# Perceiver block on one core: the order and the semaphores of the first loads, and the first norms group by group

## The reference, cut to what matters

```python
x = x + L0_xattn(_layernorm(x), ctx_1024, ...)   # self attention, cross attention, feed forward
x = x + L0_attn(_layernorm(x), ...)
x = x + L0_ffn(_layernorm(x), ...)
x = x + L1_xattn(_layernorm(x), ctx_1024, mask, ...)
x = x + L1_attn(_layernorm(x), ...)
x = x + L1_ffn(_layernorm(x), ...)
```

```python
scores = einsum('bhqd,bhkd->bhqk', q, q) / sqrt(128)
scores = where(among the 5 largest of the row, scores, -inf)
out = merge_heads(softmax(scores) @ q) @ self_out_w.T + self_out_b
x = layernorm(x + out) * ln1_g + ln1_b
```

## Time and profile before

| | |
|---|---|
| median of 3 runs | 3657.43 us (3654.14 to 3657.65) |
| the profiled execution, its own time | 3659.62 us |
| its span, first to last instruction | 3656.9 us |
| busy: PE, DVE, ACT, POOL | 92%, 69%, 52%, 31% of the span |
| mean granted TensorE clock | 0.958 |
| first instruction of DVE, PE, ACT | 15.86, 22.95, 24.24 us |

### The profile page before, as it was taken

How to read it: one execution, slowest core, us unless ns; L and a number is a source line. 1 busy time by engine, 2 the same in 40 slices (tenths; PEclk the granted TensorE clock), 3 DMA queues, 4 the chain that set the end, 5 groups by cost and what they waited for, 6 DMA issues and landing times. The chain is left out here.

```text
span 3656.9 us, 83216 instructions
## 1 busy us (share of the span) xinstructions
PE 3368.5 (92%) x32913; PEld 2372.4 (65%) x32913; DVE 2508.6 (69%) x7162; ACT 1895.5 (52%) x2944; POOL 1145.4 (31%) x807
## 2 busy tenths in 40 slices
PE   6879999999997787999999999999999998957998
PEld 4646666666665665777777777777777776634555
DVE  5657777778785444777777777777777776675333
ACT  4336666666664222666666666666666664522332
POOL 1043333333331003433444334443344431233000
PEclk9969999999999688999999999999999999978999
DMA  1023333333330011111111111111111101000000
GB/s 52 2 68 75 81 71 76 76 78 73 75 65 1 2 47 41 42 33 35 37 42 42 33 36 37 42 42 33 30 42 42 42 22 47 1 27 1 1 1 12
DMA packets 95125, 146.43 MB, mean 40 GB/s; under 512 B 14961, under 2 KB 72337, under 8 KB 93969
## 3 DMA queue, kind: packets, MB, share of 16 engines
q1 hardware_dynamic: 94736, 141.12, 14.4%
HBM read 100.66 MB, written 1.05 MB: 28 GB/s over the span
## 5 line engine op out<-in xcount | busy, mean ns | idle before, releaser
L2137 DVE SCALAR_TENSOR_TENSOR arena<-banks,arena 128x512 f16<-128x512 f32 (+1 forms) x1024 | 554.4, 583 | 309.2 <-ACT arena L2226 307.9
L2226 ACT ACTIVATE arena<-banks 128x512 f16<-128x512 f32 (+1 forms) x1024 | 471.4, 512 | 399.5 <-PE banks L2044 396.4
L1092 DVE TENSOR_REDUCE arena<-banks 128x1 f32<-128x512 f32 (+1 forms) x896 | 529.1, 627 | 187.1 <-PE banks L977 181.8
L1189 ACT ACTIVATE arena<-banks 128x1024 f32<-128x1024 f32 (+1 forms) x448 | 425.0, 964 | 315.1 <-PE banks L998 312.2
L2149 DVE CUSTOM_DVE_ANT_0 arena<-banks,arena 128x1024 f32<-128x1024 f32 (+1 forms) x512 | 494.3, 987 | 31.0 <-issue 30.7
L2233 ACT ACTIVATE arena<-arena 128x1601 f32<-128x1601 f32 x256 | 417.7, 1632 | 107.3 <-DVE arena L2155 105.3
L2044 PE MATMUL banks<-consts,arena 128*128 128x128 f32 (+1 forms) x3328 | 457.6, 276 | 7.4 <-DVE arena L2137 6.6
L2058 PE MATMUL banks<-arena 128*128 128x256 f16 (+1 forms) x1664 | 456.2, 274 | 0.7 <-ACT arena L2240 0.7
L2060 PE MATMUL banks<-arena 128*128 128x256 f16 (+1 forms) x1664 | 451.3, 271 | 0.0
L2059 PE MATMUL banks<-arena 128*128 128x256 f16 (+1 forms) x1664 | 450.2, 271 | 0.0
L2044 PEld LDWEIGHTS banks<-consts,arena 128*128 128x128 f32 (+1 forms) x3328 | 365.6, 141 | 17.6 <-issue 10.5
(11 more groups left out here) (364 smaller groups left out, 6144.6 us busy)
## 6 DMA issues: line engine op xcount, KB each, us to landing
arena<-in_ctxT SPq DMA_DIRECT2D x64, 800.5 KB, 4.5
arena<-arena SPq DMA_DIRECT2D x768, 50.0 KB, 2.2
arena<-in_ctx SPq DMA_DIRECT2D x32, 768.0 KB
arena<-in_mask SPq DMA_DIRECT2D x32, 200.1 KB, 4.5
arena<-in_m2w SPq DMA_DIRECT2D x3, 2048.0 KB, 8.4
arena<-in_xw SPq DMA_DIRECT2D x1, 2048.0 KB, 11.6
weights<-in_weights SPq DMA_DIRECT2D x1, 1920.0 KB, 7.7
arena<-in_ctx SPq DMA_DIRECT2D x32, 32.5 KB
```

The source lines that it names most:

```text
L1092: eng.tensor_reduce(o, s, AX, ALU.max).then_inc(a_max, 1)
L1189: eng.activation(pr[0:w, at % 4, :].rearrange("p (x n) -> p x n", x=2)[:, :, 0:n], c.ps[0:w, bank:bank + 2, 0:n], ACT.Exp, scale=scale).th ...
L2137: eng.scalar_tensor_tensor(out=part(ptl, g, gr), in0=turned(gr), scalar=TOP, in1=part(pth, g, gr), op0=ALU.mult, op1=ALU.subtract).then_in ...
L2226: eng.activation(part(pth, g, gr), turned(gr), ACT.Copy, scale=TOP).then_inc(t_high, 1)
```

## The change

It issues the loads in another order, `x` first and in two parts (pairs 0 to 3, then 4 to 15), then `consts`, `rows`, `weights`; gives each part of `x` and `consts` a semaphore of its own; takes the loads out of the `after` list; lets DVE wait for the two parts of `x`, PE for `consts` ahead of its first loop and for `rows` and `weights` ahead of the first projection; and interleaves DVE's statistics and norms: statistics of group g, then the norms of group g - 1.

```diff
-        c.loaded = ctx.enter_context(nc.semaphore("inputs_loaded"))
+        c.loaded = ctx.enter_context(nc.semaphore("weights_rows_loaded"))
+        c.x_loaded = [ctx.enter_context(nc.semaphore(f"x_loaded{n}")) for n in range(2)]
+        c.consts_loaded = ctx.enter_context(nc.semaphore("consts_loaded"))
...
     def sp(eng):
+        x = A["x"].rearrange("(i b) l d -> (b l) i d", b=2)
+        eng.dma_start(c.x[:, 0:G, :], x[:, 0:G, :]).then_inc(c.x_loaded[0], 16)
+        eng.dma_start(c.x[:, G:PAIRS, :], x[:, G:PAIRS, :]).then_inc(c.x_loaded[1], 16)
+        eng.dma_start(c.c[:], A["consts"]).then_inc(c.consts_loaded, 16)
+        eng.dma_start(c.r[:], A["rows"]).then_inc(c.loaded, 16)
         eng.dma_start(c.w[:], A["weights"]).then_inc(c.loaded, 16)
-        eng.dma_start(c.r[:], A["rows"]).then_inc(c.loaded, 16)
-        eng.dma_start(c.c[:], A["consts"]).then_inc(c.loaded, 16)
-        eng.dma_start(c.x[:], A["x"].rearrange("(i b) l d -> (b l) i d", b=2)).then_inc(c.loaded, 16)
...
-    m.after = [(c.loaded, 64), (constant, 5)]
+    m.after = [(constant, 5)]
...
         def project(g):
             eng.wait_ge(s["oT"], g + 1)
+            if g == 0:
+                eng.wait_ge(c.loaded, 32)
...
+        eng.wait_ge(c.consts_loaded, 16)
         for g in range(GROUPS):
             bank = 4 + g % 2
...
     def dve(eng):
-        norms.dve_stats(eng, lambda i: c.x[:, i, :])
-        for g in range(GROUPS):
-            norms.dve_apply(eng, g, lambda i: c.x[:, i, :], lambda i: xn[:, i, :])
+        for g in range(GROUPS + 1):
+            if g < GROUPS:
+                if g < 2:
+                    eng.wait_ge(c.x_loaded[g], 16)
+                norms.dve_measure(eng, g, lambda i: c.x[:, i, :])
+            if g > 0:
+                norms.dve_apply(eng, g - 1, lambda i: c.x[:, i, :], lambda i: xn[:, i, :])
```

## The result

The changed kernel took 3638.96 us (median of 5 runs, 3636.83 to 3640.58), the kernel before 3655.78 us (5 runs, 3649.94 to 3657.65): ratio 0.9956, 95% interval 0.9943 to 0.997, so 16.8 us less, with an interval of 11 to 21 us. Forecast were 13.5 us less and 3643.9 us; the time lies inside the range of 3638.5 to 3649.5, but only 0.5 us above its low end. The profiled execution took 3640.58 us at a span of 3638.8.

What follows compares the result with a forecast made beforehand. The start was taken to bound what the change can move: loads, POOL's memsets and operations, DVE's norm, then PE. PE's first transposes ending at 10.66 instead of 24.14 gave 13.5 us, from 3657.43 to 3643.9 us, range 3638.5 to 3649.5.

Steps and rivals of the forecast that it cites:

- The path: Start: all loads 15.8 us, POOL's memsets 5.27, POOL's operations and way to DVE 1.33, DVE's norm 0.49, PE at 22.98.
- The last lands at 15.8 again, count back: Loads at the start: same bytes, last landing 15.8; counted back, consts 9.5, x's second part 7.15, its first 4.55.
- a DMA more costs nothing: Loads at the start: splitting x adds one DMA, price bounded by nothing and 0.43 us, taken as nothing.
- a short first load would put everything behind it back by 1.0 us: Loads: estimate from the skill page, x's first part taking 1.9 us, everything behind 1.0 us later, gain that much less.
- POOL's memset under the loads: POOL's start: memsets begin at about 1.1, are not slowed by loads, and are over at 6.4.
- the two limits: PE's start: consts at 9.5 and group 0's norms (8.84 first, 9.57 fourth) meet within 0.1 us.
- The waits in project: First projection: rows and weights landed by 15.8, matmul with rows at 81, new wait costs nothing, 65 us to spare.
- What follows moves as a block, except for the clock: After the start: everything 13.5 us earlier; PE's clock stretches of 1.64 us, two more or fewer, plus or minus 3.3 us.
- 1 (loads together): Loads share the engines and land together near 15.8: only 4.3 us less, 3653.1 us; chance 0.06.
- 3 (a bad start of the loads): Short first DMA holds back those behind by 2 to 6 us: gain 7.5 to 11.5 us, 3646 to 3650; chance 0.06.
- 2 (the clock against it): PE falls into more 1.2 GHz stretches; over 8 eat the gain, 13 give 3665.2 us; chance 0.02.
- 4: PE still needs rows and weights at the start, so the gain is 4.3 us; given no chance of its own.

Runs made afterwards that it cites:

- E1: The changed kernel, but POOL again waits for all loads before it clears the values' buffer; 3653.26 us, ratio 1.0002 to the kernel before.
- E4: The changed kernel with x loaded in one DMA; 3642.95 us in one profiled execution.
- E10: The changed kernel with consts split, its first-needed part loaded behind x's first part, group 0's norms and factor sooner, ACT's table load early; 3636.23 us, ratio 0.9955.
- E12: E10 with 25 filler matmuls, read by nothing, on PE at the end of self attention; 3634.63 us, ratio 0.9949 to the kernel before.
- E8: The changed kernel run once more, unaltered, for its profile; 3642.0 us in one profiled execution.
- E11: The changed kernel a third time, unaltered, for time and profile; 3638.70 us, ratio 0.996 to the kernel before.
- E7: The kernel before run once more, unaltered, for its profile; 3650.83 us in one profiled execution.
- E2: The changed kernel with loads in the old order (weights, rows, consts, x's two parts), semaphores and interleaving kept; 3649.91 us, ratio 0.9989.
- E3: The changed kernel without interleaving: statistics of all four groups, then the norms; 3640.98 us in one profiled execution.
- E6: The changed kernel with 60 matmuls of zeros on PE ahead of its wait for consts; 3644.95 us, ratio 0.9974 to the kernel before.

## Why the prediction was right, point by point

- **The path** (loads, POOL's memsets, POOL's operations, a norm, PE): right. E1 shows it: with POOL's wait for the loads put back, 0.5 us of the lead are left.
- **The loads.** "The last lands at 15.8 again, count back": right, consts at 9.3 for 9.5. The first part of x came 0.8 us earlier than counted (3.7 for 4.55), its second 0.6. That a DMA more costs nothing held for x: E4, with one less, had consts at 9.7 and the last load at 15.9, no earlier than the kernels with two parts (8.6 to 9.7 and 15.2 to 15.8). It does not hold for every split: in E10 and E12, with a sixth load of 194 KB, the last one landed at 16.9 and 17.4. Whether the number of loads or the narrow part of consts makes that is open.
- **The pages on loads.** The Trainium skill's "DMA: Bandwidth & Descriptors", sections "Bandwidth" and "Rules for kernel authors", from which the prediction estimated that a short first load would put everything behind it back by 1.0 us, is not borne out for the 256 KB at the head of the queue: consts at 9.3 is 0.2 us before the 9.5 counted without such a cost. E10 and E12 go the way of its rule, with 1.4 and 1.9 us. The rule in its section "Two DMAs through the same engine are not ordered", that nothing orders DMAs across engines, was not contradicted, but in every profile here the loads landed in the order of issue.
- **POOL's memset under the loads**: 3.94 us, unslowed, and the end of all three at 6.3: right.
- **DVE**: group 0's norms at 7.75 for 8.35, in step with x's earlier landing. In the first profile they ended 0.5 us before consts landed, and in E8 too PE was held by consts. In E11 x's second part landed at 7.0, the norms ran from 8.24 to 9.33, and PE was held by them until 9.41, with consts landed at 9.3. So the two limits do lie close together, as the prediction said, and which one comes last changes from execution to execution.
- **PE**: 9.31 for 9.55, 13.76 us of lead at ACT for the 13.5 of the sum (13.64 and 13.66 in E8 and E11). The term is right to 0.3 us.
- **The waits in project**: L609 ran at 79.59 with no wait for a load.
- **"What follows moves as a block, except for the clock"**: right in kind. The clock was given plus or minus 3.3 us, from two stretches at 1.64 us. The price holds in the loop (1.6 us again, the tail's first part), but it isn't the price everywhere: in the last projection and the turn behind it such a stretch costs 3.3 us. There PE works longer at the lower level, and all that it loses is passed on: from the turn of the heads to DVE's statistics 7.14 us in place of 4.26 (179.15 to 186.29, 161.91 to 166.17), and 0.46 in the last turn. The scatter was also sized too small: single executions of the same kernel differ by 7 us in self attention alone (E7), and by 12 and 15 us in the whole (19 runs from 3647.27 to 3659.24, 23 runs from 3649.58 to 3664.45; three runs within 3.5 us were too few to read it from). For the difference of two medians plus or minus 3.3 us was just enough.
- **3638.96 against 3643.9**: 1.65 of these 4.9 us come from the kernel before, whose median fell from 3657.43 to 3655.78 with two more runs; for that the range had 2 us. The other 3.3 us are 16.8 in place of 13.5 us of gain, within the measured interval of 11 to 21. Two terms at their limits left the time 0.5 us inside the range, which is luck as much as foresight. E11 gives 15.1 us. Whether the changed kernel also meets fewer slow stretches on average stays open: its three profiles show 161.8 to 166.9 us from PE's first matmul to the end of self attention, those of the kernel before and E1 162.3 to 169.4, overlapping, and nothing was run that would settle it. In E2 the time gained, 3.9 us, was less than the lead at the start, 5.4.
- **Rivals**: 1 (loads together) is refuted by E2. 3 (a bad start of the loads) didn't come. 2 (the clock against it) didn't come; it needed over 13.5 us in the median, and while single executions of one kernel spread by up to 15 us, the medians of the kernel before differ by at most 2.6 us over four sets of runs. 4: all waits were as the order showed.

Parts of the lead by the runs, in us at PE's first matmul, each as what is lost when it alone is undone: POOL free of the loads 13.1 (E1), order of the loads 8.3 (E2), split of x 1.4 (E4), interleaving 1.0 (E3). They don't add up, since they stand on one path. One part was not undone by itself: PE's first wait without rows and weights. By an estimate from the landings it is worth some 6 us, since the last load came at 15.5 and PE began at 9.31.

## What to carry to other kernels

A common "everything is loaded" wait also holds engines that need none of it: look at what each engine does first behind it. Here the largest part was POOL's wait, ahead of a memset that needed no load. Count the landings back from the last one and ask for each load who needs it first; and before a gain of a few us is judged, read from several executions how much the same kernel scatters, and at which point of the timeline the lead is made.

## What the runs showed of the hardware that was not expected

- In its first stretch PE ran at half speed (four transposes 1.16 us against 0.60) while the window's granted clock read 1.00: in these profiles that column says nothing before the first recorded change of level, and the durations have to be read in its place.
- SP's issue of the load behind x took 1.21 us in the changed kernel, 0.91 and 0.85 in E1 and E3 and 2.10 in E4, where x is one DMA, against 0.43 for a load behind others. Here the landings didn't suffer, as earlier loads were still under way. An engine with other work behind such an issue would presumably be held; no run here has that.
- PE working on zeros from 1.1 us on reached 2.4 GHz between 5 and 7 us (its windows show 11 instructions in 3 to 5 us, 13 in 5 to 7 and 20 in 7 to 9), and was back at half at 24.0 us, where four transposes took 1.11 us, after a wait of 2.99 us for ACT (E6).
- One stretch at 1.2 GHz costs 1.6 us in the pair loop (the earlier trace rows and the tail's first part, 18.61 against 17.01) and 3.3 us in the last projection with its turn (15.05 against 11.71), where PE's longer times are passed on whole.
